# Convolution phase: three of eight tap stages summed by VectorE at addresses from registers

## The chip, the cores and the metric

The kernel runs on one core of a Trainium2 chip. The metric is the device time of one execution in microseconds (us), lower is better. Engines are TensorE (PE, with its weight loads as PEld), VectorE (DVE), ScalarE (ACT), GpSimd (POOL) and SyncE (SP), which here issues the DMAs.

## The reference

The program computes x + conv(layernorm(x)), then x + ffn(layernorm(x)), then an attention layer, then the feed-forward layer again. Only the convolution is touched:

```
x: (2, 512, 256), block_values: (128, 64, 64, 16), cols, rows: (128,) in 0..7
xb = layernorm(x).reshape(2, 8, 64, 256)
for each block n: o[n] = causal conv over t (16 taps) of xb[:, cols[n]] with block_values[n]
y[:, rows[n]] += o[n]            # 128 blocks fall on 8 x 8 pairs (col, row)
x = x + y
```

In the draws used here, cols and rows lie in 0..3 (they are drawn for 256 channels), so that only 16 of the 64 pairs occur. Blocks that fall on the same pair may be added before the convolution; that is what both versions do: the sum over blocks of the weights for each of the 64 pairs and 16 taps, then a convolution with the summed weights. Products are made in a split form: each fp32 operand is a rounded high part and a low part (the difference), and three products high·high, low·high, high·low are added up.

## The kernel before

Four phases follow each other, each a block of its own in which every engine has its own instruction list: `conv_phase`, `ffn_phase`, `attention_phase`, `ffn_phase`. At the end of a block the engines meet.

In `conv_phase` the 16 taps are eight stages of two taps (NST = 8). The 128 partitions of the weights hold, for the sum, the 128 blocks; after the sum, two taps times 64 input channels. For each stage:

- SyncE loads the stage's raw weights in halves of 2 MB into four buffers `raw` (L196 for the first four, in ten pieces; L201 in a loop for the other twelve, each behind a wait for the sums that read the buffer before).
- TensorE (`sum_blocks`, L377) adds the blocks with a one-hot matrix (128 blocks x 64 pairs, built from cols and rows) as the moving operand: for each of 64 output channels it loads a 128x128 weight tile and streams 64 columns; eight channels fill one PSUM bank, and four banks take turns, eight fillings a stage. In fp32 each of these is two instructions.
- ScalarE rounds each bank to `ws_hi` (L223), VectorE subtracts to get `ws_lo` (L300) and so frees the bank. Both have two slots, one for even and one for odd stages.
- TensorE (`convolve`, L388) makes 24 matmuls of 128x512 into the accumulators in banks 4 to 7. A second set of products for channel blocks 4 to 7 stands in a branch on `flag` (any column or row of 4 or more) that isn't taken here.

TensorE's order is sums of stage 0 and 1, then convolve(i), sums of stage i + 2, and so on, and convolve(6), convolve(7) at the end. Beside this, the input is loaded twice to `x_dup` (L190), normalised by VectorE (L310, L313, L323) with the power from GpSimd (L268), rounded by ScalarE (L213, `round_input`) and split by VectorE and GpSimd (L245, `split_input`); the first convolve waits for it. Matmuls on zeros (L354, `open_accumulators`) open the accumulators and keep TensorE busy: WARM = 56 of them before the first sum and two behind each of the first 16 bank sums. Behind the last convolve VectorE adds the accumulators to X (L339) and takes statistics for the next phase; L57 is TensorE's filler at the end.

## Time and profile before

| | |
|---|---|
| time, median of 3 runs | 977.54 us (977.53 to 977.71) |
| the profiled execution | 977.77 us, span 976.0 us, 1.7 us around it |
| convolution phase | 0 to 182.2 us of the span |
| TensorE busy | 98% of the span |
| VectorE, ScalarE, GpSimd busy | 51%, 44%, 32% |
| granted TensorE clock | full in all 40 slices |
| bytes moved | 63 MB, of which 33.5 MB raw convolution weights |

Times in a timeline are us from the span's start. The duration of a matmul contains its pipeline, so the rate of a series is read from start to start. "Idle before" names what ended the idle time of the engine.

### The profile page before, as it was taken

How to read it: one execution, taken by the hardware profiler on the slowest of the kernel's cores; microseconds unless marked ns; L12 is line 12 of the kernel's file. 1: busy time of each engine (PE TensorE's matmuls, PEld its weight loads, DVE VectorE, ACT ScalarE, POOL GpSimd, SP SyncE). 2: the span in 40 equal slices, each digit the busy share in tenths (PEclk: the TensorE clock that was granted, in tenths of full speed). 3: DMA queues.
4: the chain of work that ended last, by engine and by line, in shares of the span. 5: the costliest groups of instructions: out<-in, count | busy, mean ns of one | idle time of the engine just before them, and what ended most of it. 6: DMA issues, size and time to landing. Idle time of an engine off the chain costs nothing. (4 is left out here: it accounts for less than half of the span.)

```text
span 976.0 us, 17610 instructions
## 1 busy us (share of the span) xinstructions
PE 956.1 (98%) x6178; PEld 832.7 (85%) x6178; DVE 496.5 (51%) x1132; ACT 431.1 (44%) x952; POOL 309.3 (32%) x268
## 2 busy tenths in 40 slices
PE   9999999999999999899999999999999999999998
PEld 5999999588888888667897898899788788888887
DVE  4722232552333333668867866876886633333333
ACT  1521222163443334346656665664672533333442
POOL 2300000125555555422112121211210245555553
PEclk9999999999999999999999999999999999999999
DMA  9956460111111111110010000000001011111111
GB/s 269 419 188 245 173 228 1 33 44 33 48 48 48 48 48 49 47 43 22 1 34 22 0 32 0 21 0 0 2 1 33 18 49 48 48 45 44 40 48 60
DMA packets 24053, 62.98 MB, mean 65 GB/s; under 512 B 2960, under 2 KB 13904, under 8 KB 21712
## 3 DMA queue, kind: packets, MB, share of 16 engines
q1 hardware_dynamic: 24016, 62.48, 19.4%
q8 instruction: 23, 0.38, 0.2%
q14 instruction: 14, 0.11, 0.0%
HBM read 61.43 MB, written 1.05 MB: 64 GB/s over the span
## 5 line engine op out<-in xcount | busy, mean ns | idle before, releaser
L791 PE MATMUL bank<-f_xt_hi,f_w_lo 128*128 128x512 f32 (+1 forms) x400 | 157.1, 393 | 0.0
L791 PE MATMUL bank<-f_xt_hi,f_w_hi 128*128 128x512 f32 (+1 forms) x400 | 156.6, 392 | 0.0
L602 POOL TENSOR_TENSOR f_scaled<-f_act,f_gate_rows 128x512 f32<-128x512 f32 (+1 forms) x90 | 113.7, 1265 | 135.2 <-ACT f_act L533 134.9
L701 DVE TENSOR_TENSOR f_h<-f_scaled,bank 128x512 f32<-128x512 f32 (+1 forms) x90 | 60.9, 676 | 183.5 <-POOL f_scaled L602 183.5
L540 ACT ACTIVATE f_h_hi<-f_h 128x512 fp32r<-128x512 f32 (+2 forms) x102 | 63.7, 624 | 184.5 <-DVE f_h L701 184.5
L791 PE MATMUL bank<-f_xt_lo,f_w_hi 128*128 128x512 f32 (+1 forms) x400 | 123.7, 390 | 0.1
L377 PEld LDWEIGHTS bank<-cv_onehot,cv_raw 128*128 128x128 f32 x1024 | 117.7, 192 | 3.3 <-issue 0.6
L377 PE MATMUL bank<-cv_onehot,cv_raw 128*128 128x64 f32 x1024 | 116.8, 274 | 0.2 <-DMA cv_raw<-in_wconv 0.2
L970 ACT ACTIVATE at_prob<-bank,at_sbias,at_qrs 128x512 f32<-128x512 f32 (+3 forms) x128 | 77.7, 617 | 85.5 <-DVE at_sbias L1140 85.5
L808 PE MATMUL bank<-f_w_lo,f_h_hi 128*128 128x256 f32 (+1 forms) x400 | 113.2, 283 | 0.0
L808 PE MATMUL bank<-f_w_hi,f_h_lo 128*128 128x256 f32 (+1 forms) x400 | 113.2, 283 | 0.0
L808 PE MATMUL bank<-f_w_hi,f_h_hi 128*128 128x256 f32 (+1 forms) x400 | 113.1, 283 | 0.0
L710 DVE TENSOR_TENSOR f_h_lo<-f_h,f_h_hi 128x512 fp32r<-128x512 f32 (+2 forms) x102 | 70.2, 688 | 73.2 <-ACT f_h_hi L540 72.9
L1039 POOL TENSOR_TENSOR at_qrs<-at_qsum,minus_half 128x4 f32<-128x4 f32 x32 | 32.8, 1024 | 208.4 <-DVE at_qsum L1096 208.4
L300 DVE TENSOR_TENSOR cv_ws_lo<-bank,cv_ws_hi 128x512 fp32r<-128x512 f32 x64 | 43.8, 690 | 94.3 <-ACT cv_ws_hi L223 94.2
L791 PEld LDWEIGHTS bank<-f_xt_lo,f_w_hi 128*128 128x128 f32 (+1 forms) x400 | 74.6, 187 | 17.2 <-DVE f_xt_lo L111 0.5
L791 PEld LDWEIGHTS bank<-f_xt_hi,f_w_hi 128*128 128x128 f32 (+1 forms) x400 | 75.1, 188 | 13.9 <-issue 0.9
L791 PEld LDWEIGHTS bank<-f_xt_hi,f_w_lo 128*128 128x128 f32 (+1 forms) x400 | 75.1, 188 | 13.1
L533 ACT ACTIVATE f_act<-bank 128x512 f32<-128x512 f32 (+2 forms) x102 | 60.0, 591 | 58.3 <-PE bank L791 58.3
L223 ACT ACTIVATE cv_ws_hi<-bank 128x512 fp32r<-128x512 f32 x64 | 38.1, 597 | 104.6 <-PE bank L377 104.5
L808 PEld LDWEIGHTS bank<-f_w_hi,f_h_hi 128*128 128x128 f32 (+1 forms) x400 | 76.4, 191 | 3.9
L808 PEld LDWEIGHTS bank<-f_w_hi,f_h_lo 128*128 128x128 f32 (+1 forms) x400 | 76.4, 191 | 3.7
(177 smaller groups left out, 2016.4 us busy)
## 6 DMA issues: line engine op xcount, KB each, us to landing
cv_raw<-in_wconv SPq DMA_DIRECT2D x12, 2048.0 KB, 7.8
f_wraw<-in_w SPq DMA_DIRECT2D x44, 256.0 KB, 2.7
cv_raw<-in_wconv SPq DMA_DIRECT2D x6, 1024.0 KB, 20.8
f_wraw<-in_w SPq DMA_DIRECT2D x44, 128.0 KB, 2.5
at_wraw<-in_wqkv SPq DMA_DIRECT2D x3, 768.0 KB, 4.5
cv_x_dup<-in_x SPq DMA_DIRECT2D x4, 512.0 KB, 8.1
cv_raw<-in_wconv SPq DMA_DIRECT2D x4, 512.0 KB, 12.5
at_oraw<-in_wo SPq DMA_DIRECT2D x4, 512.0 KB, 3.5
```

The costliest lines, as they stand in the source:

```text
L223: a.activation(ws_hi[slot][:, :, o0:o0 + OB], ps[bk][:].rearrange("p (w o) -> p w o", o=OB), ACT.Copy)\
L300: v.tensor_tensor(ws_lo[slot][:, :, o0:o0 + OB], ps[bk][:].rearrange("p (w o) -> p w o", o=OB), ws_hi[slot][:, :, o0:o0 + OB].bitcast(F32) ...
L377: m = t.matmul(ps[bk][:].rearrange("p (w o) -> p w o", o=OB)[:, :, o], raw[2 * slot + h][:, w0:w0 + P], onehot[:], start=True, stop=True)
L533: a.activation(act[half][0:rows, cols], pg[half][0:rows, cols], ACT.Silu).then_inc(s["act_done"], 1)
L540: a.activation(h_hi[slot][0:rows, cols], h_f[half][0:rows, cols], ACT.Copy).then_inc(s["h_hi_done"], 1)
L602: g.tensor_tensor(scaled[half][:, cols], act[half][:, cols], gate_rows[:, half * HALF + cols.start:half * HALF + cols.stop], ALU.mult).the ...
L701: v.tensor_tensor(h_f[half][0:rows, cols], src[half][0:rows, cols], pu[half][0:rows, cols], ALU.mult)\
L710: v.tensor_tensor(h_lo[slot][0:rows, cols], h_f[half][0:rows, cols], h_hi[slot][0:rows, cols].bitcast(F32), ALU.subtract).then_inc(s["h_lo ...
L791: mm = t.matmul(bank[half][0:rows, :], w, x, start=q == 0, stop=q == len(steps) - 1)
L808: mm = t.matmul(bank, h[hslot][0:rows, tok], w, start=first and q == 0 and j % 2 == 0, stop=last and q == 2, skip_group_check=True)
L970: a.activation(prob[:, sl, POFF[j]:POFF[j + 1]], ps[bank][:, col:col + n], ACT.Exp, bias=sbias[:, sl, j:j + 1], scale=qrs[:, sl, j:j + 1], ...
L1039: p.tensor_tensor(qrs[:, u % 2, :], qsum[:, u % 2, :], pm["minus_half"][:, 0:NQ], ALU.pow)\
```

## The change

Stages 0 to 4 are still summed by TensorE. The sums of stages 5, 6 and 7 are made by VectorE in SBUF: a new tile `acc` holds 64 pairs x 192 values (3 stages x 64 channels) on 128 partitions; for each of 128 blocks VectorE adds the block's 192 values to the place of its pair, as two additions of 96, with the address taken from a register. The pair numbers are worked out once in a row of 128 integers (`line_pair`) and loaded eight at a time. These blocks come in a layout of their own (`wtaps`, 16 pieces of 8 blocks, 0.79 MB each) into three buffers that share their place with `x_dup`. The adds stand between the bank splits of stages 2, 3 and 4: two pieces ahead of stage 2, one ahead of stages 3 and 4, and one behind each two banks. Then ScalarE and VectorE split `acc` straight into `ws_hi` and `ws_lo`, in four pieces a stage.

Also changed: raw weights of TensorE's stages come in twenty pieces of 1 MB into three buffers instead of sixteen of 2 MB into four; the first two of them are loaded ahead of the input; GpSimd fills `acc` with zeros in two halves; the zero matmuls are 22 ahead of the sums and none between the banks; the loops over stages are written out; `convolve` ends with a one-column matmul that frees the slot.

```
+NPE, ND = 5, 3
+CO, OB, DB = 16, 8, 8
-        WARM = 56
+        WARM = 22
@@ sync
+            def blocks_first(c):
+                if c >= 3:
+                    sp.wait_ge(s["summed"], (c - 2) * CB)
+                sp.dma_start(raw[c % 3][:], ins["wconv"][c]).then_inc(raw_in[c % 3], 16)
+            def taps_first(d):
+                if d >= 3:
+                    sp.wait_ge(s["added"], 2 + 2 * DB * (d - 2))
+                else:
+                    sp.wait_ge(s["xc_lo_v"], 1 if d == 0 else B)
+                    sp.wait_ge(s["xc_lo_g"], 1 if d == 0 else B)
+                sp.dma_start(raw_d[d % 3], ins["wtaps"][d].rearrange("p (n f) -> p n f", n=DB)).then_inc(raw_d_in[d % 3], 16)
...
+            for q in range(CB):
+                part = slice(q * CHUNK // CB, (q + 1) * CHUNK // CB)
+                sp.dma_start(raw[0][:, part], ins["wconv"][0][:, part]).then_inc(first_in[q], 16)
+            blocks_first(1)
...
+            input_copies(0)
+            blocks_first(2)
+            blocks_first(3)
+            input_copies(1)
+            for c in range(4, 8):
+                blocks_first(c)
+            taps_first(0)
+            blocks_first(8)
+            taps_first(1)
+            taps_first(2)
+            blocks_first(9)
+            blocks_first(10)
+            taps_first(3)
+            for c, tail in ((11, (4,)), (12, (5,)), (13, (6,)), (14, (7, 8)), (15, (9,)), (16, (10,)), (17, (11,)),
+                            (18, (12, 13, 14)), (19, (15,))):
+                blocks_first(c)
+                for d in tail:
+                    taps_first(d)
@@ scalar
+            def round_sums(st):
+                a.wait_ge(s["ws_free"], st + 1)
+                a.wait_ge(s["added"], 2 + 2 * NBLK)
+                for q in range(PIECES):
+                    a.activation(ws_hi[slot][:, q * PW:(q + 1) * PW, :],
+                                 acc[:, q * PW:(q + 1) * PW, e * BS:(e + 1) * BS], ACT.Copy).then_inc(s["ws_hi_done"], 1)
+            round_banks(0, range(0, 8))
+            round_banks(1, range(0, 1))
             round_input(0, 0)
+            round_banks(1, range(1, 2))
             round_input(0, 1)
+            round_banks(1, range(2, 4))
             round_input(1, 0)
+            round_banks(1, range(4, 5))
             round_input(1, 1)
+            round_banks(1, range(5, 8))
@@ gpsimd, ahead of each rstd
+                g.memset(acc[:, b * NW // 2:(b + 1) * NW // 2, :], 0.0).then_inc(s["acc_zeroed"], 1)
@@ vector
+            def low_sums(st):
+                for q in range(PIECES):
+                    v.wait_ge(s["ws_hi_done"], splits_before(st) + q + 1)
+                    v.tensor_tensor(ws_lo[slot][:, q * PW:(q + 1) * PW, :],
+                                    acc[:, q * PW:(q + 1) * PW, e * BS:(e + 1) * BS],
+                                    ws_hi[slot][:, q * PW:(q + 1) * PW, :].bitcast(F32),
+                                    ALU.subtract).then_inc(s["ws_lo_done"], 1)
+            def add_blocks(d):
+                _, pairs = nc.values_load_multi_w_load_instructions(line_pair[0:1, d * DB:(d + 1) * DB], engines=[mybir.EngineType.DVE], min_val=0, max_val=NW - 1,
...
+                v.wait_ge(raw_d_in[d % 3], 16 * (d // 3 + 1))
+                for n in range(DB):
+                    for k in range(2):
+                        v.wait_ge(s["added"], (d * DB + n) * 2 + k + 1)
+                        part = slice(k * DROW // 2, (k + 1) * DROW // 2)
+                        dst = acc[:, bass.ds(pairs[n], 1), part].rearrange("p a f -> p (a f)")
+                        v.tensor_tensor(dst, dst, raw_d[d % 3][:, n, part], ALU.add).then_inc(s["added"], 1)
...
+            low_banks(0, range(0, 2))
+            statistics(0)
+            variances(0)
+            low_banks(0, range(2, 4))
...
+            low_banks(0, range(4, 6))
+            normalize(0)
+            low_banks(0, range(6, 7))
+            statistics(1)
+            variances(1)
+            low_banks(0, range(7, 8))
+            low_banks(1, range(0, 1))
+            normalize(1)
+            low_banks(1, range(1, 2))
+            split_input(v, 0, 0, s["xc_lo_v"])
+            low_banks(1, range(2, 5))
+            split_input(v, 1, 0, s["xc_lo_v"])
+            low_banks(1, range(5, 8))
...
+            for st in range(2, NPE):
+                for _ in range(2 if st == 2 else 1):
+                    add_blocks(d)
+                    d += 1
+                for q in range(0, SB, 2):
+                    low_banks(st, range(q, q + 2))
+                    add_blocks(d)
+                    d += 1
+            for st in range(NPE, NST):
+                low_sums(st)
@@ tensor
+            def convolve(st):
+                t.wait_ge(s["ws_lo_done"], splits_before(st + 1) if st < NPE else splits_before(st) + PIECES // 2)
+                for c in range(NCB // 2):
+                    for r in range(GC // 2):
+                        products(st % 2, c, r, st * 2)
+                t.wait_ge(s["ws_lo_done"], splits_before(st + 1))
+                high_products(st)
+                t.matmul(ps[4][:, 0:1], zeros[:, 0:P], zeros[:, 0:1], start=False, stop=False)\
+                 .then_inc(s["ws_free"], 1)
...
+            for st in range(NPE - 2):
+                convolve(st)
+                sum_blocks(st + 2)
+            for st in range(NPE - 2, NST - 1):
+                convolve(st)
+            convolve_last(NST - 1)
```

## Rows read from the trace of the kernel before

**Rows 1.** Page, engine shares, and granted TensorE clock in 40 slices.

```profile
PE 956.1 (98%) x6178; PEld 832.7 (85%) x6178; DVE 496.5 (51%) x1132; ACT 431.1 (44%) x952; POOL 309.3 (32%) x268
...
PEclk9999999999999999999999999999999999999999
```

**Rows 2.** Busy time by stretch: stretch, busy us (count) by engine, PEclk, DMA share, GB/s.

```profile
3.00:13.00 10.00, 10.00 (x43) 4.07 (x42) 0.95 (x7) 0.00 (x0) 0.00 (x0) 1.00 1.10 204
14.00:30.00 16.00, 15.82 (x126) 13.78 (x124) 14.90 (x55) 7.24 (x8) 3.29 (x2) 1.00 1.02 417
...
56.40:70.30 13.90, 13.90 (x127) 13.90 (x125) 4.82 (x7) 4.18 (x7) 0.00 (x0) 1.00 0.47 173
```

**Rows 3.** Groups by line, convolution: busy us, mean ns, then idle before and its releaser.

```profile
L377 PE MATMUL bank<-cv_onehot,cv_raw 128*128 128x64 f32 x1024 | 116.8, 274 | 0.2 <-DMA cv_raw<-in_wconv 0.2
L300 DVE TENSOR_TENSOR cv_ws_lo<-bank,cv_ws_hi 128x512 fp32r<-128x512 f32 x64 | 43.8, 690 | 94.3 <-ACT cv_ws_hi L223 94.2
```

**Rows 4.** Timeline, TensorE: start us, us, engine, line, operation, count, idle before.

```profile
1.20 3.60 PE L354 MATMUL bank<-zeros 128*128 128x512 bf16 x8 [1.20 <-DVE zeros L278]
...
4.85 11.05 PE L354 MATMUL bank<-zeros 128*128 128x512 bf16 x48
16.08 1.97 PE L377 MATMUL bank<-cv_onehot,cv_raw 128*128 128x64 f32 x16 [0.18 <-DMA cv_raw<-in_wconv]
...
50.57 0.59 PE L388 MATMUL bank<-cv_xc_hi,cv_ws_hi 128*128 x1
```

**Rows 5.** Timeline, TensorE, same columns: two later stages, then the phase's end.

```profile
76.26 14.40 PE L377 MATMUL bank<-cv_onehot,cv_raw 128*128 128x64 f32 x128
...
96.11 14.40 PE L377 MATMUL bank<-cv_onehot,cv_raw 128*128 128x64 f32 x128
...
182.23 1.03 PE L57 MATMUL bank<-zeros 128*128 128x512 bf16 x4
```

**Rows 6.** Timeline, VectorE, start of the convolution and one of its later stages.

```profile
14.92 2.71 DVE L310 BATCH_NORM_STATS2 cv_stats<-cv_x_dup 128x6 f32<-128x256 f32 x8 [9.82 <-DMA cv_x_dup<-in_x]
...
23.65 2.67 DVE L323 TENSOR_SCALAR cv_x_dup<-cv_x_dup,cv_moments,cv_rstd 128x256 f32<-128x256 f32 x8
...
32.00 4.85 DVE L245 TENSOR_TENSOR cv_xc_lo<-cv_x_dup,cv_xc_hi 64x2048 fp32r<-64x2048 f32 x1
36.77 1.27 DVE L300 TENSOR_TENSOR cv_ws_lo<-bank,cv_ws_hi 128x512 fp32r<-128x512 f32 x2
37.97 2.27 DVE L245 TENSOR_TENSOR cv_xc_lo<-cv_x_dup,cv_xc_hi 64x2048 fp32r<-64x2048 f32 x1
```

**Rows 7.** Timeline, ScalarE and GpSimd, start of the convolution.

```profile
28.83 1.91 ACT L213 ACTIVATE cv_xc_hi<-cv_x_dup 64x2048 fp32r<-64x2048 f32 x1
...
1.45 0.30 POOL L257 MEMSET cv_xc_hi<- 128x240 f32 x1
...
38.06 5.86 POOL L245 TENSOR_TENSOR cv_xc_lo<-cv_x_dup,cv_xc_hi 64x2048 fp32r<-64x2048 f32 x1 [3.35 <-ACT cv_xc_hi L213]
```

**Rows 8.** VectorE, one line: duration ns least/median/most, first and last start.

```profile
L660 DVE TENSOR_TENSOR f_prob<-f_lexp,f_lrec x2: 294/294/294, 204.2 to 770.5; 128x128 f32<-128x128 f32 x2
```

**Rows 9.** Timeline, VectorE: small operations that follow each other without a wait.

```profile
208.08 0.16 DVE L671 MATCH_REPLACE8 f_rest<-f_top,f_prob 128x18 f32<-128x18 f32 x1
208.16 0.08 DVE L671 MATCH_VALUE_LOAD f_rest<-f_top,f_prob 128x8 f32 x1
```

**Rows 10.** Register instructions by line: duration ns least/median/most, first and last start.

```profile
L415 PEldq TENSOR_LOAD <-cv_any_high x1: 484/484/484, 48.6 to 48.6; - x1
L415 PEldq FUSED_REGOPS  x1: 175/175/175, 49.2 to 49.2; - x1
...
L331 DVEq FUSED_REGOPS  x3: 78/84/84, 51.2 to 131.4; - x3
L331 DVEq ALU_OP  x3: 40/40/40, 91.3 to 170.9; - x3
```

**Rows 11.** DMA issues, 0 to 60 us: count, KB each, median us to landing.

```profile
cv_raw<-in_wconv SPq DMA_DIRECT2D x4, 2048.0 KB, 10.5
```

More of the change, by code:

```diff
@@ L214, in round_input, with round_banks @@
                              ACT.Copy).then_inc(s["xc_hi_done"], 1)
-            def round_stage(st, slot, banks=range(2 * BANKS)):
+            def round_banks(st, banks=range(SB)):
+                slot = st % 2
                 if 0 in banks:
@@ L306, in _ @@
[L306 to L309 removed]
+                    v.wait_ge(s["ws_hi_done"], st * SB + q + 1)
+                    v.tensor_tensor(ws_lo[slot][:, :, q * OB:(q + 1) * OB],
+                                    ps[q % BANKS][:].rearrange("p (w o) -> p w o", o=OB),
+                                    ws_hi[slot][:, :, q * OB:(q + 1) * OB].bitcast(F32),
+                                    ALU.subtract).then_inc(s["ws_lo_done"], 1)
@@ new lines, in add_blocks @@
+            def add_blocks(d):
+                _, pairs = nc.values_load_multi_w_load_instructions(
+                    line_pair[0:1, d * DB:(d + 1) * DB], engines=[mybir.EngineType.DVE], min_val=0, max_val=NW - 1,
+                    skip_runtime_bounds_check_because="columns and rows are numbers of channel blocks, 0 to 7 each")
+                v.wait_ge(raw_d_in[d % 3], 16 * (d // 3 + 1))
+                for n in range(DB):
+                    for k in range(2):
+                        v.wait_ge(s["added"], (d * DB + n) * 2 + k + 1)
+                        part = slice(k * DROW // 2, (k + 1) * DROW // 2)
+                        dst = acc[:, bass.ds(pairs[n], 1), part].rearrange("p a f -> p (a f)")
+                        v.tensor_tensor(dst, dst, raw_d[d % 3][:, n, part], ALU.add).then_inc(s["added"], 1)
@@ L310, in _, with statistics, variances @@
+            def statistics(b):
+                v.wait_ge(xd_in[b], 32)
+                for n in range(b * NCB, (b + 1) * NCB):
                     v.bn_stats(stats[:, n, :], x_dup[:, b, n % NCB, :]).then_inc(s["stats_done"], 1)
-                for n in tiles:
+            def variances(b):
+                for n in range(b * NCB, (b + 1) * NCB):
                     v.wait_ge(s["stats_done"], n + 1)
@@ L388, in products, with high_products @@
                     t.matmul(ps[4 + r][:], lhs, rhs, start=False, stop=False)
-            def convolve(st, slot, last=False):
-                t.wait_ge(s["ws_lo_done"], (st + 1) * 2 * BANKS)
+            def high_products(st):
                 with t.If(flag != 0):
@@ L411, in _, with convolve_last @@
+            def convolve_last(st):
+                t.wait_ge(s["ws_lo_done"], splits_before(st + 1))
+                high_products(st)
+                for r in LAST_ORDER:
+                    if r < GC // 2:
+                        for c in range(NCB // 2):
+                            products(st % 2, c, r, st * 2)
+                    t.matmul(ps[4 + r][:], zeros[:, 0:P], zeros[:], start=False,
+                             stop=True).then_inc(s["conv_done"], 1)
             t.wait_ge(s["onehot_ready"], 1)
@@ L422, in _ @@
-            for u in range(2):
-                convolve(NST - 2 + u, u, last=u == 1)
+            t.wait_ge(s["xc_lo_v"], B)
+            t.wait_ge(s["xc_lo_g"], B)
+            for st in range(NPE - 2):
[4 more added lines that the diff above has]
+            convolve_last(NST - 1)
             keep_busy(t, pm, ps[1], 8)
```

192 lines of the change are left out of this document (84 added, 108 removed).

## Prediction

> **What bounds the kernel now.** I read the page first: TensorE is busy 98% of the span and its granted clock is full in all slices [rows 1]. So time goes away only where TensorE's work goes away, and only as far as no other engine takes its place. The groups by line then show where the convolution's TensorE time lies: L377, the sums of blocks, has 1024 instructions and waited 0.2 us in all; VectorE's split L300 spent 94 us waiting [rows 3]. VectorE worked 4.8 us of the 13.9 us of a stage's sums [rows 2]. The timeline gives the rates: one stage (sums and one convolve) takes 96.11 - 76.26 = 19.85 us, of which the sums 14.3 (1.79 a bank, eight banks) and the convolve 5.56 [rows 5]. The convolution begins its first convolve at 50.57 [rows 4] and ends at 182.23, where L57 starts [rows 5]. Nothing behind that point is changed, and what SyncE prefetches for the next phase is issued long before it in both versions, so I work out that point alone.
>
> **Part 1, the start.** The first sum begins at 16.08, when its raw weights land behind 2.1 MB of input [rows 4]. Now they are ahead of it, and only 14 zero matmuls at 11.05/48 = 0.23 us stand behind 4.85: it begins at about 8.2. The 32 zero matmuls between banks go as well, 0.2 us each. Without waits the sums of two stages would end at 8.2 + 16 x 1.75 = 36. DMA doesn't allow that: 204 GB/s while the input copies run, 417 later [rows 2], so 2.1 MB of input and 8.4 MB of weights take 10.3 + 20.1 us from about 3 us on, and the last piece must wait besides until a buffer is free (three instead of four); it lands near 35, and its sums follow two pieces later, at about 41. The input has a chain of its own: second copy in at about 24, statistics 3.3, power 1.7 (an estimate, small GpSimd work), normalising 2.7 [rows 6]; then ScalarE's four roundings of 1.9 each stand in its list between banks of stage 1, the last ending near 39.5, and GpSimd's split of it takes up to 5.9 [rows 7], VectorE's between 2.3 and 4.9 [rows 6]. First convolve at 44.5 (41 to 47), against 50.57: 6 us gained. GpSimd's two memsets of 6144 values at 0.30/240 us a value [rows 7] are at most 7.7 us each; the first ends before the input lands, the second fits between the two powers (about 19 to 27) and is needed at 27.6: nothing, or 1 us if it is late.
>
> **Part 2, what TensorE loses.** Three stages of sums, 3 x 14.3 = 42.9 us. If it were never held up: 44.5 + 3 x 19.85 + 5 x 5.56 + 0.8 for the closing matmuls = 132.7.
>
> **Part 3, what VectorE gets.** 16 pieces of 8 blocks, each a register load and 16 adds of 96 values. An add of 128 values from SBUF lasts 0.294 [rows 8], but what counts is start to start. Two splits of 512 values take 1.27 where one lasts 0.69, so 0.58; eight of 256 take 2.67, 0.33 each [rows 6]; operations of 18 values follow after 0.08 [rows 9]. That is a line of 1.0 ns a value over 0.06: 0.16 for 96 values. The semaphore chain reaches back two adds, so it asks for half of an add's 0.26 plus a signal, less than 0.16. An address costs the sequencer a register operation of 0.04 to 0.084 [rows 10] beside the 0.08 of a small instruction: 0.12 to 0.165. I take 0.17 an add, 2.7 us a piece. The load has one row, one value in 0.48 with a register operation of 0.18 behind it, on TensorE [rows 10]. Bounds for eight values: below, all of it under adds still queued, 0; above, eight times the row, 3.9 + 0.2 = 4.1. It is nearest to the single row: 0.66, and seven more registers at a register operation's 0.08, makes 1.2, nothing hidden. Piece: A = 3.9 us.
>
> The Trainium skill, Runtime: NRT & Kernel Launch, section Instruction fetch mechanics, gives a load about 200 ns a register; by that eight would be 1.6 us, A would be 4.3 and the end 6 us later. No row here has more than one register.
>
> In the list of VectorE each piece stands ahead of bank splits, and TensorE may be only four banks ahead of them, with ScalarE behind TensorE. Two banks and a piece are 2 x 0.62 + 3.9 = 5.1 us for VectorE, 3.6 us for TensorE, which rests 5.56 us more a stage while convolving: 24.6 against 19.85 a stage. So VectorE is the bound of stages 2 to 4, and TensorE waits. From 45.0: 16 x 3.92 = 62.7, 24 splits of 0.62 = 14.9, and about 0.9 of waiting for the first banks of stage 2: last add at T = 123.5. TensorE has done convolve(4) by then.
>
> **Part 4, the tail.** Behind T: ScalarE rounds 1024 values a partition (half of the 2048 in 1.91 [rows 7]: 1.0), VectorE splits them (1.1 by the line above), the second piece is through at T + 3.4, where convolve(5) starts. It ends at T + 9.0 and frees the slot of stage 7; four roundings and the last split make T + 14.6, by which convolve(6) is done as well; convolve(7) with its closing matmuls takes 6.3: T + 20.9 = 144.4. In general the end is 81.7 + 16 A, but not under 132.7.
>
> **Part 5, DMA.** From 44.5 on 11 pieces of 1.05 MB and 15 of 0.79 MB have to come, 23.3 MB, 56 us at 417 GB/s: until about 103, before T. A piece of half the size of the 2 MB ones, 10.5 us median then [rows 11], should land sooner. SyncE's list mixes both kinds, so a wait for "added" holds weights for TensorE back behind it and the other way round; with VectorE as the bound each wait is met a few us before the piece is used. I cost it at nothing; if it gave way to 300 GB/s, the end would be 154.
>
> **Sum.** 182.2 - 144.4 = 37.8 us. The profiled execution is 977.77 (976.0 and 1.7 around it), 0.2 above the median: 940.0.
>
> **Rivals.**
> (a) TensorE stays the bound: load hidden or cheap, A under 3.2. End 132.7: 928. For it, register instructions run beside queued operations; against it, a load has to be done before the next address, and only small adds cover it. 0.22.
> (b) Adds don't overlap. If each waits for the one before to be written out, it costs 0.26 instead of 0.17, A = 5.3, end 166.5: 962. Rows 9, with 0.08 between operations of 0.16, speak against it; that those were other operations, with no register in their address, for it. With it goes a dearer load, A between 4.8 and 6.3: 0.16 together.
> The Trainium skill, VectorE: DVE Perf Modes, section The DRAIN you can't avoid, says that the next operation doesn't start until the pipeline is empty, and the section on the errata advises tiles of 512 and more. That is rival (b) and speaks against this change; rows 6 and 9 show starts before the end of the operation in front.
> (c) Slower than before: eight values are loaded one after the other, each at the row's 0.48. Place: ahead of each of 16 pieces, with VectorE the bound. A = 2.7 + 4.1 = 6.8, end 190.5: 986. It decides from A = 6.3 on. 0.09.
> (d) TensorE rests in stages 2 to 4, its clock falls, and the last three convolves run slower. The first eight zero matmuls take 3.60 us, 0.45 each, against 0.23 later [rows 4], although the granted clock reads full; at that rate the tail would be up to 16 us longer: 944 to 956. In stages 2 to 4 it would only use up waiting. 0.05.
> (e) DMA is late as in part 5: 950. 0.05.
> (f) The change doesn't bring its own bound since a code path differs (an extra check or copy per address): in A, covered by (b) and (c).
>
> **How the numbers follow.** Forecast A between 3.2 and 4.8, 0.43: 929 to 954, likeliest 940. (a) 0.22, (b) 0.16, (c) 0.09, (d) 0.05, (e) 0.05. Range 925 to 966: 925 takes in (a) with the first convolve at 41; 966 takes in (b)'s 962; left out are (c), the upper part of (b) and a start earlier still, under 0.2. A measurement of this kernel tells about 0.2% (2 us) from no change. Faster 0.89, same 0.02, slower 0.09.
>
> **What would show it.** In the profile after: first L377-like sum at about 8, first convolve at 44.5 (part 1); adds of 96 values 0.16 to 0.17 apart and a hole of about 1.2 us ahead of every sixteenth (part 3; 0.26 apart means (b), a hole of 4 means (c)); TensorE's sums held by VectorE's split in stages 2 to 4, its busy share under 90% there (no such waits means (a)); 21 us from the last add to the end; DMA waits of TensorE or VectorE short. Wrong would be above all a load whose hole isn't 0.3 to 2 us, since each 0.1 us of A is 1.6 us of time.

## The result and the profile after

Median 954.03 us (953.19 to 954.07) against 977.62 us (977.53 to 977.8) of the kernel before on the same chip: ratio 0.9756, 95% interval 0.9739 to 0.9773, so 23.6 us faster. The profiled execution has a span of 952.3 us; line numbers from here on are those of the changed kernel. The forecast was 940.0, so the sign and the range hold, and the likeliest time is 14 us too low (that it is no more is luck, as the part on the prediction works out). The page says first that something is different in kind: TensorE no longer has its full clock everywhere. Its parts: busy time and share by engine, then granted clock in 40 slices of 23.8 us.

```profile
PE 921.9 (97%) x5735; PEld 801.5 (84%) x5735; DVE 547.7 (58%) x1378; ACT 428.2 (45%) x940; POOL 319.3 (34%) x270
...
PEclk9679979999999999999999999999999999999999
```

Against [rows 1], TensorE has 443 instructions fewer but only 34 us less busy time, and slices 2, 3 and 6 read 6, 7 and 7. Groups by line of the convolution (busy us, mean ns, idle before and releaser) show the same:

```profile
L477 PE MATMUL bank<-cv_onehot,cv_raw 128*128 128x64 f32 x640 | 89.2, 312 | 6.3 <-DMA cv_raw<-in_wconv 6.3
...
L377 DVE TENSOR_TENSOR cv_acc<-cv_acc,cv_shared 128x96 f32 x256 | 51.8, 254 | 3.4 <-DVE cv_acc L377 2.5 <-issue 0.6
...
L353 DVE TENSOR_TENSOR cv_ws_lo<-bank,cv_ws_hi 128x512 fp32r<-128x512 f32 x40 | 26.3, 683 | 23.5 <-ACT cv_ws_hi L266 23.5
```

The 640 sums that are left (L477, the L377 of [rows 3]) take 312 ns in the mean where 1024 took 274. No sum waited for VectorE: the only waits named are 6.3 us of DMA. VectorE, however, had nothing to spare: from 71.4 to 126.5 us not one of its bank splits (L353) waited for ScalarE. The timeline of TensorE (start us, us, then the instruction; idle before in brackets) puts it in order of time:

```profile
8.62 0.19 PE L462 MATMUL bank<-ones,cv_high 128*1 128x1 f32 x2 [3.82 <-DVE cv_high L345]
8.74 5.74 PE L456 MATMUL bank<-zeros 128*128 128x512 bf16 x14
14.31 14.40 PE L477 MATMUL bank<-cv_onehot,cv_raw 128*128 128x64 f32 x128
31.99 27.57 PE L477 MATMUL bank<-cv_onehot,cv_raw 128*128 128x64 f32 x128 [3.28 <-DMA cv_raw<-in_wconv]
59.32 0.77 PE L486 MATMUL bank<-cv_xc_hi,cv_ws_hi 128*128 128x512 f32 x1
...
66.11 14.48 PE L477 MATMUL bank<-cv_onehot,cv_raw 128*128 128x64 f32 x128
...
86.19 10.91 PE L477 MATMUL bank<-cv_onehot,cv_raw 128*128 128x64 f32 x96
97.53 3.79 PE L477 MATMUL bank<-cv_onehot,cv_raw 128*128 128x64 f32 x32 [0.42 <-DMA cv_raw<-in_wconv]
...
106.81 10.98 PE L477 MATMUL bank<-cv_onehot,cv_raw 128*128 128x64 f32 x96
120.41 7.09 PE L477 MATMUL bank<-cv_onehot,cv_raw 128*128 128x64 f32 x32 [2.62 <-DMA cv_raw<-in_wconv]
```

Stage 0's 128 sums take 14.40 us; the same 128 of stage 1, behind an idle stretch of 3.28, take 27.57; the last 32 of stage 4, behind one of 2.62, take 7.09 where 32 take 3.6 to 3.8 elsewhere. The windows name the cause (stretch, busy us and count by engine, granted clock, DMA share, GB/s):

```profile
14.30:28.70 14.40, 14.40 (x129) 14.26 (x127) 9.77 (x26) 5.35 (x8) 5.75 (x2) 1.00 0.90 244
32.00:59.00 27.00, 27.00 (x127) 27.00 (x127) 16.31 (x37) 11.71 (x11) 11.45 (x3) 0.50 0.46 167
59.00:61.50 2.50, 2.50 (x8) 2.11 (x8) 0.69 (x1) 0.60 (x1) 0.00 (x0) 0.50 1.02 428
61.50:64.00 2.50, 2.50 (x12) 1.96 (x12) 2.48 (x13) 0.00 (x0) 0.00 (x0) 0.96 1.03 435
110.00:117.70 7.70, 7.70 (x70) 7.65 (x68) 7.65 (x35) 2.39 (x4) 0.00 (x0) 1.00 0.80 281
120.40:127.20 6.80, 6.79 (x32) 6.79 (x33) 6.52 (x27) 0.60 (x1) 0.00 (x0) 0.50 0.84 289
```

Granted 0.50 is the lower level, 1.2 GHz. TensorE is fully busy from 32 to 59 us and makes half the progress; it is back at full clock some 2.5 us into the first convolve. A page that reads "PE 97%" hides this, and the busy column of the window too: only the clock column and the duration of equal work tell it. And the clock column alone can mislead: it reads full before some 14 us, but the 14 zero matmuls at 8.74 take 5.74 us behind the 3.82 us of idle time. In run e2 below they take 5.91, and there the window from 9.2 to 14.7 reads 0.50; in e6, with no idle time in front of them, they take 3.20.

The convolution ends with TensorE's last matmul at about 158.6 (its last result is added at 158.78); before it was 182.2. These 23.6 us are the whole gain, as the prediction set out to compute.

What made the start late is on VectorE and GpSimd (timeline, same columns):

```profile
3.42 4.50 DVE L336 CAST cv_colrow_f<-cv_colrow 128x2 f32<-128x2 int32 x1 [2.27 <-DMA cv_colrow<-in_rows]
3.50 4.45 DVE L338 CAST cv_pair_iota_f<-cv_pair_iota 128x64 f32<-128x64 int32 x1
...
26.41 5.75 DVE L397 TENSOR_SCALAR cv_shared<-cv_shared,cv_moments,cv_rstd 128x256 f32<-128x256 f32 x8
```

```profile
2.68 5.22 POOL L319 MEMSET cv_acc<- 128x6144 f32 x1
...
24.55 5.22 POOL L319 MEMSET cv_acc<- 128x6144 f32 x1
```

A cast of 2 and one of 64 values end when GpSimd's memset of the accumulator ends, at 7.9; the eight normalizing instructions, 2.67 us in [rows 6], take 5.75 under the second memset.

Then the adds, on VectorE's timeline (stage 2) and by line (duration ns least/median/most, first and last start):

```profile
71.38 3.23 DVE L377 TENSOR_TENSOR cv_acc<-cv_acc,cv_shared 128x96 f32 x16
74.53 1.28 DVE L353 TENSOR_TENSOR cv_ws_lo<-bank,cv_ws_hi 128x512 fp32r<-128x512 f32 x2
75.73 3.22 DVE L377 TENSOR_TENSOR cv_acc<-cv_acc,cv_shared 128x96 f32 x16
78.87 1.28 DVE L353 TENSOR_TENSOR cv_ws_lo<-bank,cv_ws_hi 128x512 fp32r<-128x512 f32 x2
```

```profile
L368 DVEq TENSOR_LOAD <-cv_line_pair x16: 594/598/847, 60.4 to 128.2; - x16
```

```profile
L377 DVEq FUSED_REGOPS  x256: 57/57/78, 61.4 to 131.9; - x128
L377 DVE TENSOR_TENSOR cv_acc<-cv_acc,cv_shared x256: 245/256/261, 61.5 to 132.0; 128x96 f32 x128
```

One load brings all eight registers in 0.60 us, and beside the two splits in front of it it leaves no hole: piece, two splits, piece repeat every 75.73 - 71.38 = 4.35 us. An add starts 0.20 behind the one before (3.23 - 0.25 over 15).

### The profile page after: what moved, and what is told of

The parts are those of the page before. It is cut to its first block and busy times, and to the rows that moved or that the text cites. A ratio compares the mean times of both kernels' runs of the same rounds, so it can differ in the third digit from the quotient of the medians.

```text
span 952.3 us, 17018 instructions
## 1 busy us (share of the span) xinstructions
PE 921.9 (97%) x5735; PEld 801.5 (84%) x5735; DVE 547.7 (58%) x1378; ACT 428.2 (45%) x940; POOL 319.3 (34%) x270
## 5 line engine op out<-in xcount | busy, mean ns | idle before, releaser
L477 PE MATMUL bank<-cv_onehot,cv_raw 128*128 128x64 f32 x640 | 89.2, 312 | 6.3 <-DMA cv_raw<-in_wconv 6.3
L477 PEld LDWEIGHTS bank<-cv_onehot,cv_raw 128*128 128x128 f32 x640 | 88.5, 227 | 6.9 <-DMA cv_raw<-in_wconv 6.7
L913 PEld LDWEIGHTS bank<-f_w_lo,f_h_hi 128*128 128x128 f32 (+1 forms) x400 | 76.4, 191 | 0.0
L694 POOL TENSOR_TENSOR f_w_lo<-f_wraw,f_w_hi 128x512 fp32r<-128x512 f32 x48 | 62.1, 1294 | 36.2 <-ACT f_w_hi L624 36.2
```

Of the source, the lines that this page charges most:

```text
L477: m = t.matmul(ps[q % BANKS][:].rearrange("p (w o) -> p w o", o=OB)[:, :, o], raw[c % 3][:, w0:w0 + P], onehot[:], start=True, stop=True)
L694: g.tensor_tensor(w_lo[slot][:, 0:n], raw_views(m, slot, rows)[0], w_hi[slot][:, 0:n].bitcast(F32), ALU.subtract).then_inc(s["w13_lo_done" ...
L913: mm = t.matmul(bank, h[hslot][0:rows, tok], w, start=first and q == 0 and j % 2 == 0, stop=last and q == 2, skip_group_check=True)
```

## The experiments

The theory formed from this: TensorE is the bound, and each of its waits of a few us costs twice, once as idle time and once as half clock behind it. Rivals: VectorE's adds set the pace; or the clock falls at these places for another reason than the idle stretch. All times are medians of four runs, with the ratio to the kernel before (977.4 to 977.6 beside each) and its 95% interval; the changed kernel is at 954.0 (0.9739 to 0.9773).

**e1_cover.** Ahead of the wait for the weights' piece 4:

```diff
+        COVER = {4: 16}
...
+                    if c in COVER and part == 0:
+                        open_accumulators(range(2 * GC, 2 * GC + COVER[c]))
                     if c > 0 and part == 0:
                         t.wait_ge(raw_in[c % 3], 16 * (c // 3 + (c % 3 > 0)))
```

> The changed kernel, with 16 matmuls on zeros (0.23 us each at the full clock) ahead of TensorE's wait for the fifth piece of raw weights, where it stood idle for 3.3 us at 28.7 and then ran at the granted clock 0.50 until about 61. Theory: the fall of the clock comes from that idle stretch; without it the sums of stage 1 take 14.4 us instead of 27.6, the first convolve starts near 46 instead of 59.3, and the time falls by 12 to 13 us to about 941. Rival 1: the sums without matmuls between them are too light, and the clock falls all the same: first convolve at 59 to 60, time 954. Rival 2: the clock stays, but the input's chain or VectorE is late by itself: first convolve at 50 or later, 945 to 948.

949.4 us (0.9718, 0.9701 to 0.9734). The timeline of TensorE, sums (here L480) and zero matmuls (L457):

```profile
27.54 3.62 PE L457 MATMUL bank<-zeros 128*128 128x512 bf16 x16
30.99 9.11 PE L480 MATMUL bank<-cv_onehot,cv_raw 128*128 128x64 f32 x80
43.69 10.51 PE L480 MATMUL bank<-cv_onehot,cv_raw 128*128 128x64 f32 x48 [3.60 <-DVE cv_ws_lo L354]
```

With the wait filled, 80 sums run at 114 ns apart, the full rate. Then comes a new wait, for VectorE, whose eight normalizing instructions lasted 6.16 us under GpSimd's split of the input, and behind it 48 sums take 219 ns each. The clock falls behind the idle stretch, wherever that lies. The first convolve starts at 53.96, not near 46, and the time is 8 us above the theory's 941.

**e2_memset_late.** GpSimd's memset waits for the two casts:

```diff
+                if b == 0:
+                    g.wait_ge(s["cr_conv"], 2)
                 g.memset(acc[:, b * NW // 2:(b + 1) * NW // 2, :], 0.0).then_inc(s["acc_zeroed"], 1)
```

> The changed kernel, with GpSimd's first memset of the accumulator behind VectorE's two small casts, which took 4.5 us each under that memset instead of 0.17. Theory: the casts block on the memset; with 0.2 us each again TensorE's first sum starts near 8.3 instead of 14.3, SyncE's fourth piece of weights, which waits for the first sums, is issued 6 us earlier and all behind it too: first convolve at 53, time 948. The idle stretch ahead of the fifth piece and the low clock behind it stay. Rival: DMA sets the start anyway, the wait for the fifth piece grows by what the sums start earlier, and the time stays within 2 us of 954.

955.1 us (0.977, 0.9754 to 0.9786). The casts are back at 0.17 and 0.19 us, but the next one-input operations, the comparison that makes the one-hot matrix and the one for the flag, now last 5.03 and 4.86. First sum at 14.97. The block had moved by two instructions, and the time is the changed kernel's within the noise.

**e3_order.** SyncE's list near its end, so that the last weights don't stand behind the tap pieces' waits:

```diff
-                            (18, (12, 13, 14)), (19, (15,))):
+                            (18, (12,)), (19, (13, 14, 15))):
```

> The changed kernel, with the last piece of TensorE's weights (number 19) issued ahead of the tap pieces 13 and 14 instead of behind them. Theory: piece 19 was held back in SyncE's list by a wait for VectorE's adds; TensorE's idle 2.6 us at 117.8 and the clock of 0.50 until 129.9 (3.3 us on two banks, 1.4 us on the convolve) go: 947 (7 us less). Rival 1: the taps come later by this and VectorE becomes late, gain under 2 us. Rival 2: the wait goes and the clock falls nevertheless, since TensorE rests elsewhere: 951.

954.3 us (0.9753, 0.973 to 0.9776). The DMA wait of 2.62 is gone, but a wait of 0.57 for VectorE is enough:

```profile
114.77 13.61 PE L477 MATMUL bank<-cv_onehot,cv_raw 128*128 128x64 f32 x64 [0.57 <-DVE cv_ws_lo L353]
```

64 sums in 13.61 is half rate over twice as many sums. What was saved in waiting was paid back in clock. The wait for VectorE is new, and it isn't this order's alone: 0.56 to 0.60 us stand at the same place, behind the first 64 sums of stage 4, in e1, e2, e5 and e6 too. TensorE may be only four banks ahead of VectorE's splits, and VectorE's list runs without a rest there.

**e4_static.** No load, fixed addresses in the adds, so that the sums of stages 5 to 7 are not the reference's; it measures time alone:

```diff
-                _, pairs = nc.values_load_multi_w_load_instructions(
...
-                        dst = acc[:, bass.ds(pairs[n], 1), part].rearrange("p a f -> p (a f)")
+                        dst = acc[:, n:n + 1, part].rearrange("p a f -> p (a f)")
```

> The changed kernel, with the adds at fixed addresses (block n of a piece always to pair n) and without the load of registers: the sums of stages 5 to 7 are not the reference's. Theory: an add is 0.20 us behind the one before because the wait for the add two back sits on the register operation in front (0.256 + 0.04 + 0.10, for two adds); without it the adds follow at 0.156 to 0.16, a piece of 16 takes 2.6 instead of 3.2, and the holes of 0.6 us between neighbouring pieces go. The end of the convolution moves by under 3 us, because TensorE sets it: 951 to 954. Rival 1: two inputs from SBUF in one place cost 0.20 by themselves, the adds stay at 0.20. Rival 2: VectorE is the bound of stages 2 to 4, and the time falls by 8 us or more.

950.8 us (0.9719, 0.9694 to 0.9744; the interval still touches the changed kernel's). On VectorE's timeline:

```profile
60.78 5.50 DVE L374 TENSOR_TENSOR cv_acc<-cv_acc,cv_shared 128x96 f32<-128x96 f32 x32
```

The adds are (5.50 - 0.25)/31 = 0.169 us apart, the 0.17 of the forecast, without a hole. A register address so costs 0.03 an add and the loads show up only between neighbouring pieces. VectorE's work is 16 x 0.45 = 7 us less at least, the end 3.4 us earlier (last result added at 155.34). That isn't by TensorE's waits for VectorE, of which there are none in either: the tap buffers come free sooner, the last weights land sooner (wait 1.43 instead of 2.62) and fewer sums run at half clock (6.08 instead of 7.09). So rival 2, VectorE as the bound with 8 us or more to gain, is out. But VectorE isn't without influence: through the tap buffers and SyncE's list its pace sets when the last weights come.

**e5_memsets, e6_memsets_cover, e7_all.** Both memsets stand behind the flag and ahead of all input work (e5); e6 adds e1's 16 zero matmuls; e7 adds e3's order and one zero matmul behind each bank of stages 3 and 4.

```diff
+            g.wait_ge(s["flag_ready"], 1)
+            for b in range(B):
+                g.memset(acc[:, b * NW // 2:(b + 1) * NW // 2, :], 0.0).then_inc(s["acc_zeroed"], 1)
             for b in range(B):
                 part = slice(b * NCB, (b + 1) * NCB)
-                g.memset(acc[:, b * NW // 2:(b + 1) * NW // 2, :], 0.0).then_inc(s["acc_zeroed"], 1)
```

> The changed kernel, with both of GpSimd's memsets of the accumulator behind VectorE's last operation ahead of the sums (the flag) and ahead of the input's statistics. In the run with the memset behind the casts only, the next two operations of one SBUF input took 5.0 and 4.9 us instead. Theory: VectorE's operations with one input from SBUF block on GpSimd's memset; with none of them beside it the first sum starts at 8.3 (14.3 before), the first normalising takes 2.7 instead of 5.75, and all of SyncE's list behind the fourth piece moves ahead by 6 us. TensorE still stands idle about 3 us ahead of the fifth piece and runs at clock 0.50 behind it: first convolve 52 to 53, time about 948. Rival: TensorE's idle time grows by the 6 us, and the time stays at 953 to 955.

953.5 us (0.9766, 0.9742 to 0.9789).

> As the run before in this list, and 16 matmuls on zeros ahead of the wait for the fifth piece of weights. With the input's chain 6 to 9 us earlier, no wait for VectorE follows in stage 1 as it did with the 16 matmuls alone (3.6 us at 40). Theory: without an idle stretch of over 1 us the clock stays full in the first 60 us: first convolve 42 to 43, and the rest as in the changed kernel, time 937 to 939. Rival: the sums by themselves lose the clock in stage 1, first convolve at 50 or later, time 945 or more.

950.2 us (0.9717, 0.9701 to 0.9733).

> As the run before, with piece 19 of the weights ahead of tap pieces 13 and 14, and one matmul on zeros behind each bank sum of stages 3 and 4 (16 in all, 3.6 us), so that TensorE's own pace there is 21.7 us a stage against VectorE's 20.65. Theory: the second fall of the clock comes from the short waits for VectorE in stage 4 (0.57 us in the run with the order changed alone, where the wait for DMA was gone and the clock fell all the same); without them the clock stays, convolve(3) takes 5.6 instead of 6.95 us and the last sums 1.8 a bank: end of the convolution at 134 to 136, time 929 to 931. Rival: the clock falls in stage 4 all the same or the matmuls on zeros cost what they save: 935 to 939.

946.7 us (0.9673, 0.9652 to 0.9693). All three fall short of their theories. In e5 the first sum starts at 8.73, as forecast for the change itself, and normalizing takes 2.66. It brings nothing: an earlier TensorE waits earlier for the same bytes (2.08 us, ending at 18.06), and all 192 sums behind that take 41.23 us at half clock. First convolve still near 59. In e6 the full clock came back during the zero matmuls at 33.3, and stage 1's 128 sums took 14.40, ending near 52. Its first convolve still starts at 55.89, behind 3.88 us of idle time. The profile names no releaser for it, but the convolve waits for both engines' splits of the input, and GpSimd's second one ends at 44.56 + 11.23 = 55.79 (timelines of TensorE and GpSimd):

```profile
55.89 0.76 PE L491 MATMUL bank<-cv_xc_hi,cv_ws_hi 128*128 128x512 f32 x1 [3.88 <-issue]
```

```profile
44.56 11.23 POOL L298 TENSOR_TENSOR cv_xc_lo<-cv_shared,cv_xc_hi 64x2048 fp32r<-64x2048 f32 x2 [8.02 <-ACT cv_xc_hi L258]
```

So with stage 1 at the full clock the input's chain is the next bound, and the clock falls behind that wait as well (0.50 from 56 to 58.5). e7 has the same there (3.74 idle, first convolve at 57.43). It has the full clock from 80 us on, and its last result is added at 152.39.

**b1_no_fill.** The kernel before without the two zero matmuls behind each of its first 16 banks, 32 x 0.23 = 7 us of work that does nothing:

```diff
-                        if use is None:
-                            open_accumulators(range(2 * GC, 2 * GC + 2))
```

> The kernel before, without the two matmuls on zeros behind each of the first 16 bank sums (6.9 us of TensorE's time). Theory: here the input is loaded first and DMA brings a bank's weights (1.2 us at 417 GB/s) faster than TensorE sums it (1.79), so TensorE has no idle stretch of over 1 us and the clock stays: first convolve at 45 to 46, set by the input's chain, time 972 to 973. Rival: TensorE waits for weights or for the input longer than before, the clock falls, and the time is 978 to 990.

985.97 us (1.0089, 1.0072 to 1.0106): slower by 8.5, where the expectation was faster. TensorE's timeline, sums:

```profile
15.69 7.33 PE L377 MATMUL bank<-cv_onehot,cv_raw 128*128 128x64 f32 x64
23.48 10.93 PE L377 MATMUL bank<-cv_onehot,cv_raw 128*128 128x64 f32 x96 [0.46 <-DMA cv_raw<-in_wconv]
36.93 20.71 PE L377 MATMUL bank<-cv_onehot,cv_raw 128*128 128x64 f32 x96 [2.52 <-DVE cv_ws_lo L300]
```

Without them a wait of 2.52 us appears, and the 96 sums behind it take 216 ns each instead of 114, with a granted clock of 0.50. So this isn't a matter of the new adds at all: the matmuls that the change removed as useless had kept TensorE behind VectorE's splits, so that no such wait arose: the sums of the kernel before waited 0.2 us in all [rows 3]. (VectorE was late there by its split of the input, 4.84 us beside GpSimd's, as the 4.85 of [rows 6].) My part 1 had booked them as a pure gain.

**e8_busy, e9_busy_input.** More cover at the start. e8: the memsets, order and later cover of e7, and at the start 20 zero matmuls ahead of piece 2, four ahead of piece 4, two behind each bank of stage 1 and eight ahead of the first convolve. e9 keeps the memsets, the order and the later cover, but at the start the second half of the input goes ahead of the weights' piece 2, and 40 zero matmuls stand ahead of piece 2, four ahead of the first convolve. e9's edit of SyncE's list:

```diff
+            input_copies(1)
             blocks_first(2)
             blocks_first(3)
-            input_copies(1)
```

> The changed kernel with the memsets late, piece 19 ahead, one matmul on zeros behind each bank sum of stages 3 and 4, and matmuls on zeros in every stretch where TensorE stood idle in the earlier runs: 20 ahead of the third piece of weights (idle 4.6 us there when the sums start at 7.7), 4 ahead of the fifth, two behind each bank of stage 1, 8 ahead of the first convolve. Nothing of the computation is changed. Theory: the whole of what the forecast missed at the start is the clock's fall behind idle stretches; with none of over 1 us the sums run at 1.8 us a bank throughout, stage 1 ends at 46 to 48, the first convolve starts at 47 to 48 (57.4 in the run with the three earlier changes) and the time is 935 to 938. Rival: the granted clock falls at 15 to 20 us with TensorE busy, first convolve at 55 or later, time 944 or more.

956.0 us (0.9781, 0.9765 to 0.9797): a miss, 2 us above the changed kernel (the intervals overlap) and 9 us above e7, from which only the cover at the start differs. Four zero matmuls didn't cover the wait for piece 4: 2.83 us idle were left, the clock fell in them, and now the fillers ran at the lower clock too, 4.16 us for a bank with its two instead of 3.5 alone.

> As the run before in this list, but with the second half of the input loaded ahead of the third piece of weights instead of behind the fourth, 40 matmuls on zeros in the longer wait for that piece, none between the banks of stage 1 and 4 ahead of the first convolve. Theory: weights now set the start alone: third piece at about 24.6, six pieces of 3.6 us, first convolve at 46 to 47, time 934 to 937, the same as the run before within 2 us. Rival: the input's chain still holds stage 1 (a wait of VectorE's splits there), the clock falls, 942 or more.

945.7 us (0.967, 0.9654 to 0.9686). No DMA wait over 0.8 us is left and the clock is full until 40.7; there TensorE waits 3.97 us for VectorE, and 48 sums take 10.50. That is the rival: the input's chain still holds stage 1.

**e10_later_fill.** Only the later stages: e3's order and one zero matmul behind each bank of stages 3 and 4.

```diff
+        FILL = {3: 1, 4: 1}
...
+                    open_accumulators(range(2 * GC, 2 * GC + FILL.get(st, 0)))
```

> The changed kernel with only the later part: piece 19 ahead, one matmul on zeros behind each bank sum of stages 3 and 4; the start is left as it is (first convolve at 59). Theory: the second fall of the clock and the wait for piece 19 are worth 6 to 7 us, less what the matmuls on zeros cost where TensorE sets the pace (1 to 2 us): time 948 to 950. Rival: nothing is gained alone, 953 to 955, because VectorE's adds end at 132 and set the end by themselves.

949.0 us (0.9709, 0.9693 to 0.9726), as expected. The window over the last sums, with 16 matmuls more than needed:

```profile
100.00:140.00 40.00, 39.84 (x248) 34.75 (x250) 37.75 (x134) 13.40 (x18) 0.00 (x0) 1.00 0.60 230
```

Full clock; last result added at 153.30, 5.5 earlier than 158.78. The order alone brought nothing (e3), the order with cover 5 us; the cover without the order wasn't run.

**e11_gp_split.** e9, with GpSimd's input splits behind VectorE's normalizing:

```diff
+            g.wait_ge(s["xn_ready"], B * NCB)
             for b in range(B):
                 split_input(g, b, 1, s["xc_lo_g"])
```

> The kernel of e9_busy_input with one wait added: GpSimd begins its two input splits only when VectorE has done both of its normalizations (64 x 2048 subtract, 3.97 us at 38.6 there, under which VectorE's eight normalize instructions took 6.17 us instead of 2.67). Theory (GpSimd's work holds VectorE's one-input instructions, TensorE waits 3.97 us for the weights' low bank at 40.7, and the granted clock falls behind that wait): normalize(1) takes 2.7 us, the wait of TensorE shrinks to under 0.6 us, the 48 sums behind it stay at the full clock (5.4 us, not 10.5), the first convolve starts at 47 to 49 instead of 57, and the run takes 936 to 939 us. Rival 1 (GpSimd's later splits then hold something else): normalize is 2.7 but the second GpSimd split ends behind 52 and the first convolve waits for it, 52 to 54; 941 to 943 us. Rival 2 (the clock falls at that place for another reason than the wait): the idle time is gone but the 48 sums take 10.5 all the same; 942 to 944 us. Rival 3 (normalize is slow without GpSimd too): nothing changes, 945.7 us.

945.0 us (0.9667, 0.9651 to 0.9683), the fastest, though not told apart from e9. VectorE (normalizing L402, its own splits L299), GpSimd's splits, and TensorE's sums L484, from their timelines:

```profile
37.84 2.67 DVE L402 TENSOR_SCALAR cv_shared<-cv_shared,cv_moments,cv_rstd 128x256 f32<-128x256 f32 x8 [0.56 <-POOL cv_rstd L325]
...
41.03 5.58 DVE L299 TENSOR_TENSOR cv_xc_lo<-cv_shared,cv_xc_hi 64x2048 fp32r<-64x2048 f32 x1
```

```profile
40.65 3.81 POOL L299 TENSOR_TENSOR cv_xc_lo<-cv_shared,cv_xc_hi 64x2048 fp32r<-64x2048 f32 x1 [2.85 <-DVE cv_shared L402]
```

```profile
41.17 2.00 PE L484 MATMUL bank<-cv_onehot,cv_raw 128*128 128x64 f32 x16 [0.48 <-DVE cv_ws_lo L358]
47.36 7.06 PE L484 MATMUL bank<-cv_onehot,cv_raw 128*128 128x64 f32 x32 [4.19 <-DVE cv_ws_lo L358]
```

Normalizing takes 2.67 again, so GpSimd's split did hold it. But then GpSimd's split runs beside VectorE's own, which takes 5.58 instead of the shorter 2.27 of [rows 6], and TensorE waits 4.19 for the bank behind it. The 2.27 wasn't undisturbed either: it started at 37.97, 0.09 ahead of a split on GpSimd [rows 7], and there it was GpSimd's that lasted long, 5.86. The other one of the kernel before:

```profile
30.89 3.82 POOL L245 TENSOR_TENSOR cv_xc_lo<-cv_x_dup,cv_xc_hi 64x2048 fp32r<-64x2048 f32 x1 [7.42 <-ACT cv_xc_hi L213]
```

This ends at 34.71, and VectorE's 4.85, begun at 32.00 beside it, ends at 36.85, 2.14 later. In e11 GpSimd's split ends at 44.46 and VectorE's, begun 0.38 behind it, at 46.61, 2.15 later. So in these rows the split that starts first takes its usual time, and the other one does its work behind it. None of my cases had this: rival 1 had a late GpSimd split holding the first convolve, and what was held was VectorE's. The wait went from one instruction to the next, as in e2.

**Idle stretches of TensorE and the clock behind them**, from the timelines and windows:

| kernel | idle us, before | granted clock behind it |
|---|---|---|
| after | 3.28 at 28.7; 2.62 at 117.8 | 0.50; 0.50 |
| e2, e3, e4, e10 ahead of stage 1 | 3.63; 3.45; 3.38; 3.20 | half rate in each |
| e1, e9, e11 | 3.60; 3.97; 4.19 | 0.50 in each |
| e5, e6, e7, e8 | 2.08; 4.64; 4.82; 2.83 | 0.50 in each |
| e6, e7 ahead of the first convolve | 3.88; 3.74 | 0.50 in each |
| e1, e2, e5, e6 in stage 4 | 0.56; 0.60; 0.58; 0.59, later 1.17; 1.25; 1.20; 1.55 | full for some 2 us, then 0.50 |
| e4 | 1.43 at 116.9 | full for over 1 us, then 0.50 |
| e3 in stage 4 | 0.57 | a mean of 0.57 in the first 2 us, then 0.50 |
| b1 | 2.52 | 0.50 |
| after, b1, e11 | 0.42; 0.46; 0.48 | stays full |
| e9, e11 behind 40 zero matmuls | 0.80; 0.75 | stays full |

All stretches of 2 us and more in this list were followed by the lower clock; so was 1.43. Of the ten short ones listed (0.42 to 0.80) five were: those of 0.56 to 0.60, all behind 64 sums in stage 4. In four of these and in e4 the fall came an interval behind the idle stretch, during sums; the waits of 1.17 to 1.55 in e1, e2, e5 and e6 lie in time that was at 0.50 already. The two of 0.75 and 0.80, which were longer and stayed full, had zero matmuls of 512 columns in front. So had the wait of 0.4 to 0.8 ahead of the last convolve, which every version of the changed kernel has and behind which the clock stayed full, a convolve's 512 columns. What decides with a short one I can't say from these runs.

## Why the prediction was right or wrong

**The bound of the sum.** That the end of the convolution alone moves held: 23.6 us of 23.6. That no other engine takes TensorE's place and that the kernel gets faster held too. That VectorE becomes the bound of stages 2 to 4 (part 3) was wrong: no sum waited for it, and that is rival (a). It was wrong by little: VectorE's splits never waited from 71.4 to 126.5, and in e1, e2, e3, e5 and e6 sums of stage 4 waited 0.56 to 0.60 for it.

**Part 3, the add and the load.** The add without a register was right (0.17, measured 0.169); with it, it is 0.20. The step that failed is the sentence on the semaphore chain, which reaches two adds back: the wait stands on the register operation of 57 ns in front of the add, not on the add. In the trace's record an add of 0.257 ends at 66.416, the register operation that waited for it starts at 66.455 and the add behind that at 66.559, so two adds take 0.257 + 0.039 + 0.104 = 0.40. The load failed by more: 0.60 for eight values and mostly hidden under the splits (all 16 loads together left the adds 3.1 us idle), against 1.2 exposed each time. The Trainium skill (Runtime: NRT & Kernel Launch, Instruction fetch mechanics) gives about 200 ns a register, for loads that the runtime puts in; here, with the eight values in SBUF, it is 0.60/8 = 0.075, one load for all. A is 3.2 + 0.6 at worst and 4.35 - 2 x 0.58 = 3.2 as it repeats, where I had 3.9; by my own formula 81.7 + 16 x 3.2 = 133, or 928, the floor. At this A the two bounds of the forecast, VectorE's and TensorE's, meet, and in the trace VectorE's list indeed ran without a rest in most of stages 2 to 4.

**Rivals (b) and (c)** didn't occur: adds that last 0.25 start 0.20 apart, and without a register 0.17. That speaks against the rule of the Trainium skill (VectorE: DVE Perf Modes, The DRAIN you can't avoid) read as a full wait for the operation in front; an exposed 0.26 was nowhere. The section itself adds that an operation that isn't held starts earlier, and with that these starts agree.

**Part 1.** First convolve at 59.3, not 44.5: 14.8 us, the largest miss. The first sum was 6 late since I cost the memset "at nothing", looking only at when its result is needed and not at whom it holds while it runs: 3.9 us came by the held casts (8.62 against 4.72 in e5 without them), and 2.5 by the 14 zero matmuls behind that idle stretch, 5.74 against 3.20. The Trainium skill (SBUF — State Buffer, Who interferes with whom) says that casts and tensor_scalar of VectorE can take a port pair shared with GpSimd, and a two-input VectorE operation contends with a GpSimd one that reads SBUF; the traces agree with both (4.50 for a cast of 128x2; 5.58 for a split). [Rows 6] had a split of 4.85 and one of 2.27, and I had used them as a spread, not asked for the cause, which is the order of the starts on the two engines (shown at e11). But e5 shows that these 6 us are worth nothing alone. What cost was stage 1 at half clock: 27.57 instead of 14.40, 13.2 us. I had expected no DMA waits that matter there and had counted the 32 zero matmuls as a gain; b1 shows that without such cover even the kernel before loses. But these 13.2 us aren't to be had alone: in e6, with stage 1 at 14.40, the first convolve came only 3.4 us earlier, since GpSimd's second split of the input ended at 55.79. That chain I had ending by about 45.

**Part 2.** A stage of 19.85 was a row at full clock without waits. From the first convolve to the end it took 99.3 us, not 88.2. The 11.1 are, against 5.56 a convolve and 14.3 for the sums: convolve(0), its first 2.5 us at 0.50, 1.2; stage 3's sums 0.6 with the DMA wait; stage 4's 20.45 - 14.3 = 6.2, of which 2.6 wait and 3.5 clock; convolve(3) begun at 0.50, 6.95, so 1.4; small differences, most of them in the last three convolves, 1.7.

**Part 4, the tail.** From the last add, which ends at 132.22, to the end are 26.4 us, not 20.9: convolve(5), due at T + 3.4, started only at 139.94, when TensorE was through with convolve(4). Here TensorE was the bound by 4 us.

**Rival (d)** named the right mechanism, TensorE rests and its clock falls, in the wrong place: behind VectorE in stages 2 to 4 and by the tail, with 0.05, "it would only use up waiting". It was behind DMA in stages 1 and 4, where sums at the lower clock were the bound; half clock cost 13.2 + 1.2 + 3.5 + 1.4 = 19 us in all. The Trainium skill (TensorE: Matmul & The Clock Gate, HAM oscillation — how this bites in real kernels) describes this pattern, waits for data that let the clock fall so that the next tile starts slow; it agrees with the table above, and I had not weighed it.

**Part 5.** DMA at nothing: 6.3 us of waits. Piece 19 was issued at 113.7 behind the wait of a tap piece in SyncE's list, though its buffer had been free since 110.4; that is the "held back by the other kind" that I named and then argued away with VectorE as the bound. The 154 for 300 GB/s (rival (e)) doesn't come out of its own numbers: 23.3 MB from 44.5 on would have landed by about 122, before T = 123.5.

So 940 was near 954 by two errors of opposite sign, which is luck: the adds 12 us too dear (144.4 against the floor of 132.7), the start and the clock 26 us too cheap (14.8 and 11.1).

**What stays open.** No run kept the full clock through stage 1 to the first convolve with all waits gone; what that would give isn't measured. e11 has VectorE's split beside GpSimd's as its last known wait of over 1 us in the convolution. How fast VectorE's list would let the kernel be is open too: in e10, at the full clock, the adds ended at 130.75 and the last result was added at 153.30.

## What to carry to other kernels

Work that does nothing may be holding the clock: before removing filler on TensorE, list the waits that it covers, and after a change read the granted clock and the duration of equal work by stretch, not the busy share. In these runs every wait of 2.08 us or more on TensorE ahead of light matmuls (64 columns, fp32) was paid again behind it, by up to 41 us at half rate; cover it with zero matmuls or move the bytes, and check that the cover is as long as the wait (e8, whose wasn't, was 9 us slower than e7). With one wait covered, look for the next: the gain of e1 was 5 us, not 13, since VectorE's wait took the place of DMA's. Cost a GpSimd operation by what VectorE starts while it runs, not only by when its result is due.

## What the runs showed of the hardware that I had not expected

- A cast of two values on VectorE lasts 4.50 us beside a GpSimd memset that started 0.74 us before it; comparisons in its place 5.03 and 4.86 (e2). In these rows the size of what is held doesn't matter, only what is left of the operation beside it. The same goes for VectorE's split of the input, and the one that starts first isn't held: 2.27 on VectorE when it starts 0.09 ahead of GpSimd's, which then takes 5.86 instead of 3.82; 4.85 and 5.58 when it starts behind it.
- At the lower clock, sums of 64 columns ran on for 27 us (after) and 41 us (e5) without the clock coming back; in the first convolve with its 512 columns it was back after some 2.5 us, in e6 during 16 zero matmuls of 512 columns. Two zero matmuls a bank didn't bring it back: e8 stays at 0.50 from 34.4 to 63.
- One register load of eight values takes 0.60 us on VectorE, one value on TensorE took 0.48 [rows 10].
